# Turning h with VectorE and 16 copies inside SBUF instead of TensorE transposes

## The reference

```
h = LN(LN(x) * pw_g[pathway] + pw_b[pathway]) * cp_g[class] + cp_b[class]
t = LN(x) * tm_g[class] + tm_b[class]
s = LN(x) * ms_g[mask] + ms_b[mask]
m, n, r = x + (LN of a two-layer network of the batch's three condition vectors)
cat = [w0 h, w1 t, w2 m, w3 n, w4 r, w5 s]        (3072 features; w = softmax(aw))
out = x + LN(silu(cat @ int_W1 + b1) @ int_W2 + b2) * int_g + int_be
```

## Time and profile before

| | before |
|---|---|
| median of 3 runs | 995.67 us (992.49 to 995.71) |
| the profiled execution's own time | 994.5 us |
| its span in the profile | 992.8 us |
| granted TensorE clock, mean | 0.995 |
| busy: PE, VectorE (DVE), ScalarE (ACT), GpSimd (POOL) | 976.8, 800.0, 272.1, 505.4 us |
| DMA: moved, mean rate | 141.70 MB, 143 GB/s |

### The profile page before, as it was taken

One profiled execution on the slowest core, in us unless ns is written; L12 is line 12 of the kernel. 1 busy time (PEld: TensorE's weight loads), 2 busy tenths in 40 slices (PEclk: granted clock), 3 DMA queues, 4 the chain that ended last, 5 costly groups with the idle time before them and its releaser, 6 DMA issues.

```text
span 992.8 us, 13724 instructions
## 1 busy us (share of the span) xinstructions
PE 976.8 (98%) x4436; PEld 802.4 (81%) x4436; DVE 800.0 (81%) x1102; ACT 272.1 (27%) x341; POOL 505.4 (51%) x624
## 2 busy tenths in 40 slices
PE   7999999999999999999999999999999999999997
PEld 6677887888888888888888888888888888888885
DVE  6986988697887979878797887879788787987855
ACT  4633232231232322132222312323122232313311
POOL 3442556375554746555374544637445474655322
PEclk9999999999999999999999999999999999999999
DMA  9953546444364553535545363554436355353122
GB/s 317 332 199 117 198 100 191 128 125 143 92 198 98 162 155 82 192 85 179 127 158 139 76 208 85 172 145 127 144 89 206 90 162 153 89 188 86 42 64 64
DMA packets 52738, 141.70 MB, mean 143 GB/s; under 512 B 10200, under 2 KB 10456, under 8 KB 48752
## 3 DMA queue, kind: packets, MB, share of 16 engines
q0 software_dynamic: 22976, 66.07, 26.4%
q1 hardware_dynamic: 29744, 75.41, 21.7%
HBM read 124.55 MB, written 16.90 MB: 142 GB/s over the span
## 4 chain that ended last, share of the span: by engine, by line
PE 84%; DVE 2%; issue 0%; POOL 0%; POOLq 0%; DVEq 0%
PE hid_ps L1327 20%; PE hid_ps L1326 20%; PE hid_ps L1325 20%; PE o_ps L1432 5%; PE o_ps L1431 5%; PE o_ps L1430 5%; PE made_ps L1305 3%; PE made_ps L1318 2%; PE hid_ps L1330 1%; DVE xc L805 0%; PE made_ps L1446 0%; DVE r_sb L943 0%; PE made_ps L1447 0%; PE made_ps L1448 0%; DVE yst L881 0%; DVE fst L927 0%
## 5 line engine op out<-in xcount | busy, mean ns | idle before, releaser
L1325 PE MATMUL hid_ps<-cat_hi,w_hi 128*128 128x512 f32 x1008 | 395.8, 393 | 0.0
L1327 PE MATMUL hid_ps<-cat_hi,w_lo 128*128 128x512 f32 x1008 | 392.9, 390 | 0.0
L1326 PE MATMUL hid_ps<-cat_lo,w_hi 128*128 128x512 f32 x1008 | 392.9, 390 | 0.0
L1325 PEld LDWEIGHTS hid_ps<-cat_hi,w_hi 128*128 128x128 f32 x1008 | 189.7, 188 | 40.1 <-issue 1.7
L1327 PEld LDWEIGHTS hid_ps<-cat_hi,w_lo 128*128 128x128 f32 x1008 | 189.5, 188 | 39.6
L1326 PEld LDWEIGHTS hid_ps<-cat_lo,w_hi 128*128 128x128 f32 x1008 | 189.6, 188 | 38.4
L490 POOL DMA_INDIRECT pw_rows<-cp,class_now x64 | 128.5, 2008 | 66.6 <-DVE y_sb L872 55.2
L659 ACT ACTIVATE cat_hi<-v_ring 128x1024 fp32r<-128x1024 f32 x64 | 68.0, 1062 | 303.3 <-DVE v_ring L854 303.2
L483 POOL DMA_INDIRECT pw_rows<-pw,path_now x64 | 98.4, 1537 | 62.1 <-DVE y_sb L890 41.5
L504 POOL DMA_DIRECT2D r_sb<-x x60 | 57.8, 964 | 109.7 <-DVE r_sb L952 99.0
L437 POOL TENSOR_TENSOR fve<-fmv,eps_col 128x1 f32<-128x1 f32 x64 | 28.5, 445 | 139.4 <-DVE fmv L909 127.1
(11 more groups left out here) (157 smaller groups left out, 1239.2 us busy)
## 6 DMA issues: line engine op xcount, KB each, us to landing
x_sb<-x SPq DMA_DIRECT2D x16, 1024.0 KB, 6.3
out<-r_sb SPq DMA_DIRECT2D x64, 256.0 KB, 2.0
xc<-xT SPq DMA_DIRECT2D x15, 1024.0 KB, 5.0
r_sb<-x POOLq DMA_DIRECT2D x60, 256.0 KB, 4.8
stats_bc<-token_stats SPq DMA_DIRECT2D x30, 256.0 KB, 5.2
ids_sb<-ids SPq DMA_DIRECT2D x16, 256.0 KB, 7.3
keep<-int_W SPq DMA_DIRECT2D x12, 256.0 KB, 7.1
w_raw<-int_W SPq DMA_DIRECT2D x12, 256.0 KB, 10.6
```

The source lines that it names most:

```text
L1325: pe.matmul(acc, w1_hi[:, k, cols], hi, start=start, stop=False)
L1326: pe.matmul(acc, w1_hi[:, k, cols], lo, start=False, stop=False)
L1327: return pe.matmul(acc, w1_lo[:, k, cols], hi, start=False, stop=stop)
```

## The change

h of batches 1 to 15 is not transposed by PE. `y_norm` writes to the second half of `pw_rows`, which y_add has read by then, `y_hat` scales it there, and VectorE turns it in squares of 32 by 32 (`y_turn`, four instructions of 128 x 512) back into `y_sb`. SP then copies the squares to their partitions, `y_sb` to `v_ring`, in 16 DMAs of 64 KB with runs of 512 bytes (`h_move`), once pair 3 has freed the slots. h_high and h_low read `v_ring`. The rows of a batch are laid over the partitions in another order to fit (`by_row`, a second input `xp`), and `xT`, the ids and the outputs lie in token order. The statistics are packed by 32 columns (`pack_cols`), turned by VectorE behind h_low(b,0) (`turn_stats`), and spread so that mean and deviation each lie in runs of 128 columns. POOL's gathers of the next rows wait for the turns and come later in its order. Batch 1 is packed by VectorE (`pack_first`), takes its four y_mul and y_add in one go, and `scaled` ahead of the centring. The last batch loads its x again in row order.

```diff
+            def h_move(b):
+                sp.wait_ge(y_turned, TT * b)
+                sp.nop(nofuse=True)
+                sp.wait_ge(used, 6 * b + 4)
+                at = slot(H0)
+                for g in range(P // 32):
+                    for a in range(P // 32):
+                        sp.dma_start(v_ring[32 * a:32 * a + 32, at:at + 2, :, g * P:(g + 1) * P].rearrange("r n k c -> r (n k) c"),
+                                     y_sb[32 * g:32 * g + 32, :, a * P:(a + 1) * P]).then_inc(h_in, 16)
...
             def spread_stats(b):
-                sp.wait_ge(x_packed, 4 * b + 2)
-                sp.dma_start(stats_dram.rearrange("v p m -> p v m"),
-                             x_pack[:, :, :, :].rearrange("p v s t -> p v (s t)")).then_inc(stats_out, 16)
+                sp.wait_ge(pack_turned, b)
+                sp.dma_start(stats_dram, pack_rows[:, :]).then_inc(stats_out, 16)
...
                 for v in range(2):
-                    sp.dma_start(stats_bc[64 * v:64 * v + 64, :, :, :].rearrange("q p s t -> q (p s t)"),
-                                 stats_dram[v].rearrange("p m -> (p m)").partition_broadcast(64)
+                    sp.dma_start(stats_bc[64 * v:64 * v + 64, :, :],
+                                 stats_dram.rearrange("(g m) i -> g (m i)", m=32)[:, v * 2 * P:(v + 1) * 2 * P].partition_broadcast(64)
                                  ).then_inc(stats_in[v], 16)
...
                 if not (first or last):
                     load_xT(b + 1)
+                if not by_pe(b):
+                    h_move(b)
                 if not first:
                     store(b - 1, 0)
...
                     sp.wait_ge(batch_rows, 1)
+                    for v in range(2):
+                        sp.wait_ge(stats_in[v], 16)
                     sp.dma_start(rows_bc[:, :, :], rows.partition_broadcast(P)).then_inc(rows_bc_in, 16)
...
             def gather(b, t):
-                wait(pool, yscaled, TT * (b - 1) + t + 1)
+                if by_pe(b - 1):
+                    wait(pool, yscaled, TT * (b - 1) + t + 1)
+                else:
+                    pool.wait_ge(y_turned, TT * (b - 2) + t + 1)
...
             def h_high(b, i):
-                act.wait_ge(filled, 6 * b + FT + i + 1)
+                if by_pe(b):
+                    act.wait_ge(filled, FT + i + 1)
+                else:
+                    act.wait_ge(h_in, 16 * 16 * b)
                 act.wait_ge(used, 6 * b + 3 + i)
-                act.activation(cat_hi[:, slot(H0 + i), :, :], made_ps[:, :, :], ACT.Copy).then_inc(h_hi_done, 1)
+                act.activation(cat_hi[:, slot(H0 + i), :, :], h_from(b, i), ACT.Copy).then_inc(h_hi_done, 1)
...
+            def turn_stats(b):
+                dve.wait_ge(x_packed, 4 * b + 2)
+                wait(dve, stats_out, 16 * (b - 1))
+                dve.transpose(pack_rows[:, :], pack_cols[:, :]).then_inc(pack_turned, 1)
...
-                mean = stats_bc[:, :, 0, :].rearrange("q p t -> q t p").unsqueeze(1).to_broadcast([P, FT, TT, P])
-                v = xc[:, :, :].rearrange("q f (t p) -> q f t p", t=TT)
-                dve.tensor_tensor(v, v, mean, ALU.subtract).then_inc(centred, FT)
+                mean = stats_bc[:, :, 0:P].unsqueeze(1).to_broadcast([P, FT, TT, P])
+                by_groups = xc.rearrange("q f (g j) -> q f g j", j=P)
+                dve.tensor_tensor(by_groups, by_groups, mean, ALU.subtract).then_inc(centred, FT)
...
+            def y_turn(b, t):
+                dve.wait_ge(yscaled, TT * (b + 1))
+                dve.wait_ge(yhat_done, TT * b + t + 1)
+                dve.transpose(y_sb.rearrange("q f (a t i) -> q (f a) t i", t=TT, i=32)[:, :, t, :],
+                              y_normed(b, t).rearrange("q (a i) -> q a i", i=32)).then_inc(y_turned, 1)
...
                 x_low(1, 0)
                 nets_weigh()
+                pack_first()
+                turn_stats(1)
                 x_low(1, 1)
                 onehot_next(1)
-                y_mul(1, 0)
-                y_mul(1, 1)
+                for t in range(TT):
+                    y_mul(1, t)
+                y_add(1, 0)
                 add_b1()
+                scaled_next(1)
                 centre(1)
-                scaled_next(1)
-                y_add(1, 0)
+                for t in range(1, TT):
+                    y_add(1, t)
...
                     y_norm(b, 2)
+                    y_norm(b, 3)
                     ts_mult(b, 2)
-                    y_norm(b, 3)
+                    y_turn(b, 0)
+                    y_turn(b, 1)
                     ts_low(b, 2)
                     out_stats(b - 1, 0, o_ps[:, 0, :])
+                    y_turn(b, 2)
+                    y_turn(b, 3)
...
                     h_low(b, 0)
+                    if not last:
+                        turn_stats(b + 1)
                     out_sum(b - 1, 2)
...
                     pair(b, 4)
-                fill_h(b, 0)
-                half_pair(b, 5, 0)
-                fill_h(b, 1)
-                half_pair(b, 5, 1)
+                    pair(b, 5)
                 second(b - 1, 3)
```

More of the change, by code:

```diff
@@ L32, with build @@
 HI, LO, AGAIN, SCL = 0, 32, 64, 16
-def build(nc, x, xT, ids, pid, small, small_at, tm_g, ms_g, rows, net_vecs, pw, cp, W1s, W2s, int_W1, int_W2, out):
+def build(nc, x, xp, xT, ids, pid, small, small_at, tm_g, ms_g, rows, net_vecs, pw, cp, W1s, W2s, int_W1, int_W2, out):
     f32, f32r, i32 = mybir.dt.float32, mybir.dt.float32r, mybir.dt.int32
@@ L308, in slot, with by_pe, by_tiles, y_normed @@
             return n % SLOTS
+        def by_pe(b):
+            return isinstance(b, int) and b < 1
+        def by_tiles(cols):
+            return cols.rearrange("q (g t i) -> q t g i", t=TT, i=32)
+        def y_normed(b, t):
+            return y_sb[:, t, :] if by_pe(b) else pw_rows[:, t, D:2 * D]
+        def h_from(b, i):
+            return made_ps[:, :, :] if by_pe(b) else v_ring[:, slot(H0 + i), :, :]
         block = ctx.enter_context(nc.Block())
@@ L408, in chunk @@
                     load_ids(b + 1)
+                if last:
+                    load_residual()
+                if not (first or last):
                     load_xT(b + 1)
+                if not by_pe(b):
+                    h_move(b)
                 if not first:
@@ L441, in x_rstd @@
             def x_rstd(b):
+                wait(pool, pack_turned, b - 1)
+                rstd(xaggr, TT * (b + 1), xve, xve_done, xrs, xrs_done, xmv, slice(0, TT), b + 1)
                 if isinstance(b, int) and b == 1:
[L444 to L448, removed]
+                    return
                 pool.nop(nofuse=True)
@@ L535, in _, with first_chunk, chunk @@
                 y_rstd(0, t)
[L537 to L545, removed]
+            def first_chunk():
+                path_ids(1)
+                gather(1, 0)
+                gather(1, 1)
+                net_rstd()
+                x_rstd(1)
+                gather(1, 2)
+                gather(1, 3)
+                class_ids(1)
+                for t in range(TT):
+                    gather_class(1, t)
+                for t in range(TT):
+                    y_rstd(1, t)
+            def chunk(b, last=False):
+                if not (isinstance(b, int) and b == 1):
                     for t in (2, 3):
@@ L550, in chunk @@
                 if not last:
+                    path_ids(b + 1)
+                    gather(b + 1, 0)
+                    gather(b + 1, 1)
+                out_rstd(b - 1, 0)
+                if not last:
                     gather(b + 1, 2)
@@ L553, in chunk @@
                     class_ids(b + 1)
-                if not first:
-                    out_rstd(b - 1, 0)
-                    add_x(b - 1, 0)
-                    out_rstd(b - 1, 1)
-                if not (first or last):
-                    x_rstd(b + 1)
-                if not first:
-                    add_x(b - 1, 1)
-                    out_rstd(b - 1, 2)
-                    add_x(b - 1, 2)
-                    out_rstd(b - 1, 3)
+                add_x(b - 1, 0)
+                out_rstd(b - 1, 1)
+                if not last:
+                    x_rstd(b + 1)
+                add_x(b - 1, 1)
+                out_rstd(b - 1, 2)
+                add_x(b - 1, 2)
+                out_rstd(b - 1, 3)
                 if not last:
@@ L567, in chunk @@
                     gather_class(b + 1, 1)
-                if not first:
-                    add_x(b - 1, 3)
+                add_x(b - 1, 3)
                 if not last:
@@ L1392, in x_low_part @@
                 if k % 2:
-                    ins.then_inc(used, 1)
-            def half_pair(b, n, half):
-                if half == 0:
-                    pair_ready(b, n)
-                for h in range(FT):
-                    ins = first_part(2 * n + half, h)
-                if half:
                     ins.then_inc(used, 1)
@@ L1561, in by_column, with by_row @@
     def by_column(ids):
```

(4 more changed lines are left out.)

114 lines of the change are left out of this document (69 added, 45 removed).

## The result

The changed kernel takes **1019.1 us** (median of four, 1017.9 to 1019.7) against 994.5 for the kernel before, measured beside it: a ratio of 1.025 (95% interval 1.023 to 1.027). It is slower by 2.5%. The prediction, 965 us with a range to 984, was wrong, and wrong in sign; what happened lies next to rival 1 (1021 us, to which it gave 0.12), but the loop has no drop of the clock, so the nearness is partly luck.

The account below looks back on a forecast made before the run. PE was taken as the bound in every loop batch. 994.5 less 26.2 (transposes) less 4.0 (step from batch 1 to 2) gave 964.3; with the median 1.2 above the profiled execution, 965 us, range 961 to 984.

Parts of the forecast that it names:

- rival 1: h's copies land late, PE stands 2 us in each loop batch and its clock drops: 1020 us, chance 0.12.
- PE as the bound, and the 26.2 us: PE bounds every loop batch; removing the transposes of 15 batches, 240 of 256, takes 26.2 us off.
- T: Time from the end of pair 3 until h has landed in `v_ring`: forecast 10.2 us, ends 7.6 and 13.5.
- VectorE: VectorE's load per loop batch, turns added, centring and `scaled` cheaper: 49.3 of 57.2 us, still not the bound.
- The move of h: SP's 16 copies per batch after pair 3: 7.1 us of issues plus 3 of landing, h there at 10.2 us.
- Contention: At h's copies: the xT load, issued one ts_mult earlier, may still be on the engines; landing taken as 3 us.
- The deadlines: Latest T without PE waiting: 13.0 us for h_low(b,1), 12.0 for the next batch's statistics, which may land at 21.9.
- the chain: Statistics of b+1, turned behind h_low(b,0), then written, issued and landed: 9.9 us after T.
- the margin of 1.8: Slack in each loop batch between T at 10.2 us and the statistics' limit of 12.0; PE waits for nothing.
- rival 2: h's copies follow one another, 1.6 us each: T 25.7, PE waits 14 us per batch, about 1180 us; chance 0.02.
- The step from batch 1 to 2: Fill(2,1)'s wait for VectorE and the slow clock behind it: all 4.0 us won back, ends 0 and 4.0.
- The start of batch 1: VectorE's earlier packing against add_b1 behind four y_mul, before PE's first pair: taken as 0, ends -1.2 and +2.1 us.

Follow-up runs that it names:

- the kernel whose T is 10.0: Against the changed kernel: SP and ACT each issue half the copies, statistics' turn ahead of h_low(b,0), POOL's gathers of tiles 2 and 3 late; 966.5 us.

## Why the prediction was wrong, point by point

- **PE as the bound, and the 26.2 us.** Right. 240 transposes went, a batch without waits takes 57.12 us, and the kernel whose T is 10.0 takes 966.5.
- **VectorE.** Right in each term: the turn 0.68 (0.75 forecast), the centring 2.29 (2.4), `scaled` 0.75; 48.64 busy per batch (49.3). The estimate by the Trainium skill ("VectorE: DVE Perf Modes", "The three transpose paths"), 5.0 us for four turns, is not borne out: 2.7.
- **The move of h: the step that failed.** "T = 0.1 + 7.1 + 3 = 10.2 us; the ends are 7.6 and 13.5." Measured 14.6. The issue is the term: 15 x 0.73 = 10.9 instead of 7.1, so +3.8; the landing behind the last issue is 3.5 instead of 3, and the first issue 0.1 later. The price came from the loads of 2 KB rows (0.47) and from the statistics' two (0.55); I took these for ends, and a copy between partitions, with four runs of 512 bytes on each, costs 0.66 with nothing beside it. Nor is the price fixed: it is 0.73 in the loop, and 0.77 to 0.89 in the means of the kernels with a second queue beside it. Eight copies took 0.85 each for twice the runs in batch 15, so part of the price goes by runs; what else of this shape costs more than a load was not taken apart. A resource that no row showed was bounded by rows of another shape. The Trainium skill's 0.95 us per 64 KB ("DMA: Bandwidth & Descriptors", "Measured (HBM→SBUF, 128 partitions, SWDGE, issued from GpSimd)"), which I cited and set aside, gave T = 15.3 and was nearer, by luck: it is the time of a transfer, summed as if the copies followed one another, and here it is mostly the issues that do.
- **Contention.** I named xT as the neighbour; halving it gave 0.5 us of T in the mean, and moving two gathers away 0.5 as well. All neighbours together are 2.4 to 2.7 us. That xT itself took 8.0 us instead of 5.0 is mostly the gathers' doing: it takes 5.5 beside the copies with the gathers late. With one queue the issuing is most of the time (10.55 of 12.0 us alone). With two, the neighbours count for more: late gathers take 1.8 us off T with the turn behind, 1.4 with it ahead.
- **The deadlines.** The statistics "may" land at 21.9: the table gives 21.8. From T to `scaled` I had 9.9 us: 10.7 in the batch above. So T might have been 11.1, not 12.0. For h_low I had 13.0: 12.3. Late by 4.4 (T) and 0.8 (the chain), less the margin of 1.8: 3.4 us per batch, where 3.6 is measured. The structure of the step was right, its prices were not.
- **Rival 1** named the place, h and the statistics. Its 4 us per batch were 2 of wait and 2 of clock; the truth is 3.6 of waits and restarts with the clock at 1.00, and 7 us of batch 1, so its 1021 is near by luck. The 1180 us of rival 2 do not follow from its own terms either: 14 waits of 13.7 us are 1157, and the rest would need a drop of the clock that it doesn't state.
- **The step from batch 1 to 2.** The 4.0 us are in, but not for the reason given. Fill(2,1) follows fill(2,0) by 6.8 us without a wait (9.0 before), because batch 1 brought PE there 5.1 us later; VectorE was later too, its ts_mult(2,0) starting at 155.28 where it was 152.44. In six other kernels with the copies fill(2,0) starts at 144.3 to 145.1, as before, and in five of them the wait is back, 1.7 to 2.5 us. The mechanism itself is right: with the move undone ts_mult(2,0) starts at 150.18 and the 4 us are won.
- **The start of batch 1.** -0.4, as taken (0). **Batch 1 itself** was not looked at, and lost 7.2 us against 50.95, its old length less the transposes. There pair 3 comes before fill 3 and ends at 113.1, but the first copy is issued at 117.67. On SP's queue the copies stand behind xT (issued 116.81), and xT waits for ts_mult(1,3), which ends at 116.78. PE is ready for h at 132.6, 14.9 us after the first issue, and h_high begins at 133.76, 16.1 us after it. With xT halved or the gathers late it begins 12.7 us after it, and batch 1 takes 52.2 and 52.9 us instead of 58.2. SP and PE, kernel after, and the clock behind it:

```profile
116.81 0.33 SPq L352 DMA_DIRECT2D xc<-xT  x1
117.67 12.43 SPq L378 DMA_DIRECT2D v_ring<-y_sb  x16
```

```profile
136.13 0.79 PE L1427 MATMUL hid_ps<-cat_hi,w_hi 128*128 128x512 f32 x1 [3.37 <-DVE cat_lo L948]
```

```profile
136.10:138.10 2.00, 1.97 (x5) 1.59 (x6) 2.00 (x4) 1.56 (x2) 0.73 (x1) 0.50 0.05 8
```

## What to carry to other kernels

Price a new DMA by rows of its own shape: an issue that costs 0.47 us for a plain load costs 0.66 to 0.73 for a copy of short runs between partitions, and 16 of them in a row are 12 us from the first issue until the last has landed. Where something small with a long chain behind it (here 32 columns of statistics) is put behind a wait, the margin of the chain counts and not that of the wait: moving one 0.2 us instruction gave 31 us. The same edit can win or lose by what stands beside it: late gathers cost 8 us with one queue, wherever the turn stood, and with two queues they gave 3 us with the turn ahead and 11 with it behind. And read means: one batch from the middle of a kernel showed 1.1 us where the loop had 0.5.

## What the runs showed of the hardware

- Copies inside SBUF in runs of 512 bytes go with a high share of the DMA engines at little throughput: share 1.14 at 238 GB/s in the kernel with two queues, against 0.91 at 286 GB/s while xT still moved. A share above 1 counts more than 16 engines can be busy, so it is a sign of load and no measure of how full they are.
- 16 such copies of 64 KB take 11.8 to 12.1 us from the first issue to their reader when issued by SP with nearly nothing beside them, and 8.7 to 9.1 when SP and ACT issue eight each.
- The granted clock stayed at 1.00 (2.4 GHz) behind waits of 1.4 us in every batch, of 1.7 us with two queues and the gathers late, and of 2.48 us at 154.44 with two queues and the turn ahead. It fell to 0.50 (1.2 GHz) behind 2.03 us before, behind 2.2 us in both kernels with one queue and the gathers late, behind 2.5 with xT halved, and behind 3.37 us in batch 1 after. The length of the wait alone does not tell which.
